# Two attention phases on one core: the parts of the softmax maxima made on VectorE instead of GpSimd, and a first phase with another lead and later fills

## The chip, the core and the metric

The program runs on one core of a Trainium2 chip. The metric is device time in microseconds (us) of one execution. The engines are TensorE (PE, matrix multiplications and transposes), VectorE (DVE), ScalarE (ACT), GpSimd (POOL) and SyncE (SP, which issues the transfers here). Each engine walks its own list of instructions in order; semaphores order them among the engines.

## The reference

Four layers work on x of 16 batches x 256 tokens x 128 features, with a context of 16 x 1601 x 128 and a condition of 16 vectors. Layer 0 is self attention with modulated layer norm and a gate, then cross attention to the normalized context, then an MLP with gelu. Layer 1 is a small mixture of experts. Layer 2 is cross attention to the normalized context. Layer 3 is self attention, cross attention and an MLP. All attention has 16 heads of 8 features:

```python
attn_w = softmax(einsum('bhqd,bhkd->bhqk', q, k) * scale, axis=-1)
attn_out = einsum('bhqk,bhkd->bhqd', attn_w, v)
x = x + gate_a[:, None] * (attn_out @ W_proj + b_proj)
...
c_attn_w = softmax(einsum('bhqd,bhsd->bhqs', q_c, k_c) * scale, axis=-1)   # 1601 keys
x = x + c_attn_out @ W_cproj + b_cproj
x = x + gate_m[:, None] * (gelu(x_norm2 @ W_mlp1 + b_mlp1) @ W_mlp2 + b_mlp2)
```

The softmax is over 256 keys in self attention and 1601 keys in cross attention, and it needs the maximum of each row of scores.

## The kernel before

The program has four stages after one another: `modulation` (condition vectors through weights), `attention_phase` "pa" (layer 0), `expert_layer` (layer 1), `attention_phase` "pb" (layers 2 and 3). Each attention phase has two streams of batches: z, self attention with 256 keys, and c, cross attention with 1601 keys. In pa each has 16 batches, and c's batch reads x after z's same batch. In pb c has 32 (16 of layer 2, 16 of layer 3), z has 16 between them.

**How a phase is ordered.** `body_plan` (L221) writes the plan of one *body*: a list of tokens, each with a position from 0 to 1, the stream and an offset in batches. `stage_list` (L314) repeats the plan body after body and drops what doesn't exist. In body b a token with offset `off` works on batch b + off + lead of its stream; the lead of c is 0, that of z 4 in pa and −4 in pb. So pa begins with bodies that hold only z's attention (batches 0 to 3, while c's first batches are being prepared), then has 12 with both, then four with c's attention alone. Every engine walks the same list, so a token's position fixes its place in each in-order queue.

**The tokens.** `S`/`T` are score matmuls (PE L890), `exp` on ACT L668, `V` the product with the values (PE L914). `M` computes scores once more, with queries on partitions, for the maxima: a matmul on PE (L927) into one of three banks (`dbank`), and a maximum along the row on DVE (L599). 60% of a batch's `M` (M_LEAD) lie in the body before its scores, the rest in the body itself; two batches' maxima are thus always in flight. When the four pairs of heads of one half are done, `Rn` follows:
- DVE reduces over the segments and negates: `negm`, 128x16 (L604).
- POOL casts it to bf16 (`mbf`, L815), copies that back to f32 (`mhl`, first part, L817) and subtracts it from `negm` (second part, L818).

Then `Rt`: PE transposes `mhl` (L935, waits for both parts), ACT writes it as bf16 rows (L728), and `mr` on SP (L526) copies these as additional rows of the stacked queries, where the score matmul subtracts the maximum. In pa `Rn` stands at positions 0.8135 and 0.3135 for z (half 0 and 1) and 0.8798 and 0.3798 for c, and `Rt` of c's half 1 at 0.4188.

**What prepares a batch.** `ldx` (L273) loads x and, where the norm is modulated, `acols`, its columns; `ln` is the layer norm (statistics on DVE L610 and L613, the rest on POOL L770 to L778); `xt` and `q` transpose it and project; `ctx`, `k` and `v` do so for the keys and values; POOL splits q and k into bf16 parts (L803 among them), and `kq` (SP L515, 12 transfers for q and 12 for k) stacks them. For c `ldx` stands at 0.700 with offset 3, `ln` at 0.080, `xt` at 0.150, `q` at 0.200 with offset 2. **What ends a batch**: `o`, `ot`, `proj`, `ln2`, `x2t`, `h` (POOL makes the polynomial of gelu in three 128x1024 instructions, L848, L850, L852), `tanh`, `gm`, `fc2`, `st` (store; z at 0.450, c at 0.600).

**Fills.** At the start of a phase DVE and POOL fill the tiles that need ones or zeros (stacked queries and keys of both streams, the values' column of ones, the output bank; DVE from L550). DVE then waits for all weights (L565) and permutes them. One semaphore counts all fills (N_SET); PE waits for it before the first token, SP before each `kq`.

Of the kernel before, what the change touches and what calls it, by code (L numbers as in the profile page):

```python
# [17 lines left out]
ALU = mybir.AluOpType  # L18
# [3 lines left out]
P = 128  # L22
# [198 lines left out]
def body_plan(streams):  # L221
# [46 lines left out]
    for s in streams:  # L268
# [4 lines left out]
        at(0.700, 3, "ldx")  # L273
        at(0.720, 0, "ldr")
        at(0.080, 2, "ln")
        if s.has_ctx:
            at(0.705, 3, "ldc")
            at(0.150, 2, "xt")
            at(0.200, 2, "q")
# [20 lines left out]
        else:  # L300
            at(0.240, 2, "xt")
# [12 lines left out]
def stage_list(streams):  # L314

    plan = body_plan(streams)
# [3 lines left out]
    for b in range(first, last + 1):  # L320
        for s, off, tok in plan:
            i = b + off + s.lead
            if 0 <= i < len(s.items):
                spec = s.items[i][0]
                if tok[0] in ("cs", "ca") and not spec.ctx_ln:
                    continue
                if tok[0] in ("ln2", "x2t", "h", "tanh", "gm", "fc2") and not spec.mlp:
                    continue
                out.append((tok, s, i))
# [6 lines left out]
def attention_phase(nc, nm, streams, cols_d, rows_d, ident_d):  # L336

    PROG = stage_list(streams)
# [36 lines left out]
    with Semaphores(nc) as sems, ExitStack() as ctx:  # L375
# [27 lines left out]
        for s in streams:  # L403
# [31 lines left out]

            s.x_in, s.a_cols, s.c_in = sem(f"{m}_x_in"), sem(f"{m}_a_cols"), sem(f"{m}_c_in")
# [13 lines left out]
        consts, ones_set, v_zero, biases = sem("consts"), sem("ones_set"), sem("v_zero"), sem("biases")  # L450
        tailed = [s for s in streams if s.last < P]
# [7 lines left out]
        N_SET = 6 * len(streams) + 4 * len(tailed) + 1  # L459

        @block.sync
        def _(sp):
# [24 lines left out]
            for tok, s, i in PROG:  # L487
                k, (spec, n), w = tok[0], s.items[i], i % 2
                if k == "ldx":
# [5 lines left out]
                    if spec.q_cols or spec.k_cols:  # L495
                        if i:
                            sp.wait_ge(a_free, a_done(("xt",), s, i - 1))
                            if s.has_ctx:
                                sp.wait_ge(a_free, a_done(("ctx", len(s.groups) - 1), s, i - 1))
                        sp.dma_start(s.acols[:], cols_d[n]).then_inc(s.a_cols, 16)  # L500
# [6 lines left out]
                elif k == "kq":  # L507
                    sp.wait_ge(ones_set, N_SET)
# [39 lines left out]
        def _(dve):  # L548
            for s in streams:
                dve.memset(s.kst[0][:], 1.0).then_inc(ones_set, 1)  # L550
                for i in range(2):
                    full = s.kt - 1 if s.last < P else s.kt
                    dve.memset(s.vaug[i][:, 0:full], 1.0).then_inc(ones_set, 1)
                    if s.last < P:
# [1163 lines left out]
```

## Time and profile before

| | us |
|---|---|
| median of 3 runs | 5723.09 (5717.75 to 5727.13) |
| the profiled execution | 5719.91 |
| its span, first to last instruction | 5718.1 |
| PE busy | 4820.5 |
| DVE busy | 3989.6 |
| ACT busy | 3680.6 |
| POOL busy | 1669.9 |

The profile counts as busy the time of instructions alone. A busy PE isn't PE at its peak, and a group's idle time is the time in which the engine stood before that group, put down to the semaphore event that ended it. The phases take about 36 to 2000 us (pa), 2000 to 2560 (experts) and 2560 to 5718 (pb) of the span.

### The profile page before, as it was taken

Reading aid. Unit: us, or ns where it says so; the run is one execution under the profiler, and the core shown is the slowest. Engines: PE = TensorE matmul, PEld = TensorE weight load, DVE = VectorE, ACT = ScalarE, POOL = GpSimd, SP = SyncE. Lnnn points to the kernel's source line nnn. Section 1 sums busy time; section 2 is a strip of 40 time slices with the busy share of each in tenths; the row PEclk is TensorE's granted clock in tenths of the full one; section 3 lists DMA queues with packets and bytes.
Section 4 is the critical chain, followed back from the end, with each engine's and each line's share of the span. In section 5 each row is a group of like instructions: output and inputs, shape, how many; then the busy total and the mean of one; then the engine's idle time right before and its main releaser. Section 6 shows DMA issues by size and latency. Waiting matters only on the chain.

```text
span 5718.1 us, 123215 instructions
## 1 busy us (share of the span) xinstructions
PE 4820.5 (84%) x47956; PEld 2303.5 (40%) x47956; DVE 3989.6 (70%) x8517; ACT 3680.6 (64%) x5027; POOL 1669.9 (29%) x2691
## 2 busy tenths in 40 slices
PE   3688888888888688876888888888888998888887
PEld 1233333333343267762333333343434443344333
DVE  3487777787777344445888787887777777777774
ACT  1366776676766444432777777777777776667666
POOL 2424334334322100013232423233222323222221
PEclk9699999999999899996999999999999999999998
DMA  1221111112110111111122111121212121111110
GB/s 42 64 61 44 51 54 50 52 46 58 44 52 26 37 30 32 32 28 57 46 59 60 55 49 56 51 64 51 64 52 59 39 59 43 50 40 51 40 44 7
DMA packets 362975, 271.11 MB, mean 47 GB/s; under 512 B 47911, under 2 KB 325002, under 8 KB 362396
## 3 DMA queue, kind: packets, MB, share of 16 engines
q1 hardware_dynamic: 362396, 263.23, 16.2%
q8 instruction: 383, 6.28, 0.5%
q14 instruction: 196, 1.61, 0.1%
HBM read 86.96 MB, written 12.78 MB: 17 GB/s over the span
## 4 chain that ended last, share of the span: by engine, by line
PE 32%; DVE 8%; ACT 6%; POOL 4%; issue 4%; SPq 0%; DMA 0%; ACTq 0%; POOLq 0%
PE pb_obank L914 12%; PE pb_dbank L927 8%; DVE pb_c_maxs L599 6%; ACT pb_probs L668 4%; PE pb_aunit L890 4%; PE pb_aunit L961 2%; PE pb_aunit L968 2%; POOL pb_c_cin L789 1%; PE pb_aunit L1001 1%; PE pb_dbank L975 1%; DVE pb_z_maxs L599 1%; POOL pb_c_hg L852 1%; PE pb_aunit L995 1%; POOL pb_c_cs_y L785 1%; ACT pb_c_ksp L712 1%
## 5 line engine op out<-in xcount | busy, mean ns | idle before, releaser
L599 DVE TENSOR_REDUCE pb_c_maxs<-pb_dbank 128x1 f32<-128x512 f32 (+1 forms) x3584 | 2048.7, 626 | 659.3 <-PE pb_dbank L927 646.6
L668 ACT ACTIVATE pb_probs<-pb_aunit 128x1024 f32<-128x1024 f32 (+1 forms) x1792 | 1756.5, 1025 | 465.3 <-PE pb_aunit L890 370.2
L599 DVE TENSOR_REDUCE pa_c_maxs<-pa_dbank 128x1 f32<-128x512 f32 (+1 forms) x1792 | 1027.6, 626 | 392.7 <-PE pa_dbank L927 387.4
L668 ACT ACTIVATE pa_probs<-pa_aunit 128x1024 f32<-128x1024 f32 (+1 forms) x960 | 942.9, 1025 | 260.4 <-PE pa_aunit L890 188.0
L927 PE MATMUL pb_dbank<-pb_c_kst,pb_c_qst 62*128 62x512 bf16 (+1 forms) x4096 | 886.5, 346 | 139.7 <-DVE pb_c_maxs L599 75.5
L914 PE MATMUL pb_obank<-pb_probs,pb_c_vaug 128*9 128x256 f32 x13312 | 893.2, 383 | 6.5 <-ACT pb_probs L668 6.3
L890 PE MATMUL pb_aunit<-pb_c_qst,pb_c_kst 64*128 64x256 bf16 x6144 | 597.9, 274 | 53.2 <-ACT pb_probs L668 21.3
L927 PEld LDWEIGHTS pb_dbank<-pb_c_kst,pb_c_qst 62*128 62x128 bf16 x4096 | 249.0, 94 | 778.8 <-DVE pb_c_maxs L599 561.0
L927 PE MATMUL pa_dbank<-pa_c_kst,pa_c_qst 62*128 62x512 bf16 (+1 forms) x2048 | 447.6, 353 | 62.8 <-DVE pa_c_maxs L599 24.2
L914 PE MATMUL pa_obank<-pa_probs,pa_c_vaug 128*9 128x256 f32 x6656 | 461.8, 393 | 1.1 <-ACT pa_probs L668 1.0
L914 PEld LDWEIGHTS pb_obank<-pb_probs,pb_c_vaug 128*9 128x9 f32 x13312 | 276.6, 90 | 377.2 <-issue 184.4
L890 PEld LDWEIGHTS pb_aunit<-pb_c_qst,pb_c_kst 64*128 64x128 bf16 x6144 | 258.5, 95 | 244.1 <-ACT pb_probs L668 80.4
L890 PE MATMUL pa_aunit<-pa_c_qst,pa_c_kst 64*128 64x256 bf16 x3072 | 299.3, 277 | 26.3 <-ACT pa_probs L668 17.0
L927 PEld LDWEIGHTS pa_dbank<-pa_c_kst,pa_c_qst 62*128 62x128 bf16 x2048 | 123.1, 94 | 391.0 <-DVE pa_c_maxs L599 255.7
L599 DVE TENSOR_REDUCE pa_z_maxs<-pa_dbank 128x2 f32<-128x512 f32 x256 | 163.9, 685 | 114.3 <-PE pa_dbank L927 112.8
L914 PEld LDWEIGHTS pa_obank<-pa_probs,pa_c_vaug 128*9 128x9 f32 x6656 | 140.3, 91 | 195.9 <-issue 101.9
L803 POOL TENSOR_TENSOR pb_c_kf<-pb_c_kf,pb_c_ksp 128x1024 f32<-128x1024 f32 x64 | 114.4, 1787 | 315.7 <-ACT pb_c_ksp L712 315.7
L890 PEld LDWEIGHTS pa_aunit<-pa_c_qst,pa_c_kst 64*128 64x128 bf16 x3072 | 128.9, 96 | 116.6 <-ACT pa_probs L668 44.3
L599 DVE TENSOR_REDUCE pb_z_maxs<-pb_dbank 128x2 f32<-128x512 f32 x256 | 164.3, 684 | 10.3 <-PE pb_dbank L927 8.7
L770 POOL TENSOR_SCALAR pb_c_rs_v<-pb_c_agg 128x2 f32<-128x2 f32 x32 | 7.9, 246 | 491.0 <-DVE pb_c_agg L613 490.9
L815 POOL CAST pb_c_mbf<-pb_c_negm 128x16 bf16<-128x16 f32 x64 | 12.7, 198 | 411.0 <-DVE pb_c_negm L604 411.0
L961 PE MATMUL pb_aunit<-pb_c_srct,pb_l_cross_wkp 128*128 128x512 f32 (+1 forms) x256 | 122.6, 609 | 7.8 <-ACT pb_probs L668 7.8
(475 smaller groups left out, 6607.0 us busy)
## 6 DMA issues: line engine op xcount, KB each, us to landing
pb_c_kst<-pb_c_ksp SPq DMA_DIRECT2D x384, 200.1 KB
pa_c_kst<-pa_c_ksp SPq DMA_DIRECT2D x192, 200.1 KB
pb_c_cin<-in_ctx SPq DMA_DIRECT2D x32, 768.0 KB
pa_c_cin<-in_ctx SPq DMA_DIRECT2D x16, 768.0 KB
moe_cin<-in_ctx SPq DMA_DIRECT2D x16, 768.0 KB
pb_c_qst<-pb_c_qsp SPq DMA_DIRECT2D x384, 32.0 KB
pa_z_qst<-pa_z_qsp SPq DMA_DIRECT2D x192, 32.0 KB
pa_z_kst<-pa_z_ksp SPq DMA_DIRECT2D x192, 32.0 KB
```

What stands on the lines that cost most here:

```text
L599: dve.tensor_reduce(dst, dbank[N % RING_D][:, 0:cnt * width].rearrange("p (s c) -> p s c", s=cnt), AX.X, ALU.max).then_inc(d_free, 1)
L668: act.activation(probs[u % RING_P][0:rows].rearrange("p a i q -> p (a i q)"), src[0:rows, :], ACT.Exp, scale=HD ** -0.5).then_inc(a_free, 1)
L712: act.activation(s.ksp[:, 0, at:at + width], src[:, 0:width], ACT.Identity, bias=w.bk[:]).then_inc(a_free, 1)
L785: pool.tensor_tensor(s.cs_y[:], s.cs_v[:], mhalf[:, 0:s.kt], ALU.pow).then_inc(s.c_p, 1)
L789: pool.tensor_scalar(s.cin[0:rows, t, :], s.cin[0:rows, t, :], s.cs_m[0:rows, t:t + 1], s.cs_y[0:rows, t:t + 1], ALU.add, ALU.mult).then_i ...
L803: pool.tensor_tensor(s.kf[:, part], s.kf[:, part], s.ksp[:, 0, part], ALU.subtract).then_inc(s.k_r, 1)
L852: pool.tensor_tensor(s.hg[:], s.hg[:], s.z[:], ALU.mult).then_inc(s.g_p, 1)
L890: ins = pe.matmul(dst[:, par * 512 + h * NQ:par * 512 + (h + 1) * NQ], s.kst[b2][lo:lo + ROWS, pair, t * P:(t + 1) * P], s.qst[b2][lo:lo + ...
L914: ins = pe.matmul(obank[32 * h4:32 * h4 + HD + 1, half * NQ:(half + 1) * NQ], s.vaug[i % 2][:, t, 4 * q + h4, :], src, start=(t == 0), sto ...
L927: ins = pe.matmul(dbank[nd[tok, s.key, i, par] % RING_D][:, col:col + width], s.qst[b2][lo:lo + MAX_ROW, p, qt * P:(qt + 1) * P], s.kst[b2 ...
L961: ins = pe.matmul(dst[:, at - t0 * P:at - t0 * P + width], w.wkp[:], src[:, at:at + width], start=True, stop=True)
L968: ins = pe.matmul(dst[0:rows, (t - t0) * P:(t - t0 + 1) * P], (s.srct if s.has_ctx else s.xmt)[:, t * P:t * P + rows], w.wv[:], start=True ...
```

## The change

Three things are changed. First, `Rn`'s cast, copy and subtraction are issued by DVE right behind `negm`, in both phases, and no longer by POOL. Second, in pa z's lead is 3 instead of 4, and c's `ldx`, `ln`, `xt`, `q` stand at 0.500, 0.620, 0.700, 0.760 with offset 2 (`late_x`); the load of `acols` becomes a token of its own, `lda`, in both phases. Third, fills are counted for each stream; the output bank comes first and PE waits for it alone, `kq` and the first `v` wait for their stream's fills, and in pa c's fills stand behind z's second layer norm on DVE and POOL. In pb only the order of the fills changes.

```diff
-def body_plan(streams):
+def body_plan(streams, late_x):
...
-        at(0.700, 3, "ldx")
         at(0.720, 0, "ldr")
-        at(0.080, 2, "ln")
         if s.has_ctx:
+            if late_x:
+                at(0.500, 2, "ldx")
+                at(0.620, 2, "ln")
+                at(0.700, 2, "xt")
+                at(0.760, 2, "q")
+            else:
+                at(0.700, 3, "ldx")
+                at(0.080, 2, "ln")
+                at(0.150, 2, "xt")
+                at(0.200, 2, "q")
+            at(0.701, 3, "lda")
             at(0.705, 3, "ldc")
-            at(0.150, 2, "xt")
-            at(0.200, 2, "q")
...
         else:
+            at(0.700, 3, "ldx")
+            at(0.701, 3, "lda")
+            at(0.080, 2, "ln")
...
# SP
                 elif k == "kq":
-                    sp.wait_ge(ones_set, N_SET)
+                    sp.wait_ge(s.filled, s.fills)
...
# DVE
+            def fill(s):
+                dve.memset(s.kst[0][:], 1.0).then_inc(s.filled, 1)
+                full = s.kt - 1 if s.last < P else s.kt
+                for i in range(2):
+                    dve.memset(s.vaug[i][:, 0:full], 1.0).then_inc(s.filled, 1)
+                    if s.last < P:
+                        dve.memset(s.vaug[i][0:SET_ROWS, full], 1.0).then_inc(s.filled, 1)
+                        dve.memset(s.vaug[i][SET_ROWS:P, full], 0.0).then_inc(s.zeroed, 1)
+                if s.last < P:
+                    dve.wait_ge(s.zeroed, 2)
+                    for i in range(2):
+                        dve.memset(s.vaug[i][SET_ROWS:s.last, full], 1.0).then_inc(s.filled, 1)
+
+            dve.memset(obank[:], 0.0).then_inc(ones_set, 1)
             for s in streams:
...
+                if s.key not in fill_late:
+                    fill(s)
...
                     dve.tensor_reduce(s.negm[half][:]..., AX.X, ALU.max, negate=True).then_inc(s.m_neg, 1)
+                    dve.wait_ge(s.m_neg, 2 * i + half + 1)
+                    if i:
+                        dve.wait_ge(a_full, a_done(("Rt", half), s, i - 1))
+                    dve.tensor_copy(s.mbf[half][:], s.negm[half][:]).then_inc(s.m_bf, 1)
+                    dve.wait_ge(s.m_bf, 2 * i + half + 1)
+                    dve.tensor_copy(s.mhl[half][:, :, :, 0, :], s.mbf[half][:]).then_inc(s.m_hl, 1)
+                    dve.tensor_tensor(s.mhl[half][:, :, :, 1, :], s.negm[half][:], s.mbf[half][:], ALU.subtract).then_inc(s.m_hl, 1)
...
+                for o in streams:
+                    if fill_late.get(o.key) == (k, s.key, i):
+                        fill(o)
...
# ACT, before the first v
+                    if i == 0 and tok[1] == 0:
+                        act.wait_ge(s.filled, s.fills)
...
# POOL: fill(s) in the same manner (the two stacked queries and the second K tile); Rn is gone
-                elif k == "Rn":
...
# PE
-            pe.wait_ge(ones_set, N_SET)
+            pe.wait_ge(ones_set, 1)
...
-    attention_phase(nc, "pa", [Stream("c", S, batches(l0_cross), 0), Stream("z", NQ, batches(l0_self), 4)], cols, rows, ident)
+    attention_phase(nc, "pa", [Stream("c", S, batches(l0_cross), 0), Stream("z", NQ, batches(l0_self), 3)], cols, rows, ident, True, {"c": ("ln", "z", 1)})
...
-    attention_phase(nc, "pb", [Stream("c", S, batches(l2_cross) + batches(l3_cross), 0), Stream("z", NQ, batches(l3_self), -4)], cols, rows, ident)
+    attention_phase(nc, "pb", [Stream("c", S, batches(l2_cross) + batches(l3_cross), 0), Stream("z", NQ, batches(l3_self), -4)], cols, rows, ident, False, {})
```

## Rows read from the trace of the kernel before

**Rows 1.** the page: busy time of each engine, its share of the span, instructions
```profile
PE 4820.5 (84%) x47956; PEld 2303.5 (40%) x47956; DVE 3989.6 (70%) x8517; ACT 3680.6 (64%) x5027; POOL 1669.9 (29%) x2691
```

**Rows 2.** --tile pa_c_mhl: engine idle before it until that releaser; us, times
```profile
  POOL pa_c_mhl L818: 45.8, 16
```

**Rows 3.** --tile pb_c_mhl: the same, second attention phase
```profile
  POOL pb_c_mhl L818: 13.9, 23
```

**Rows 4.** --timeline, TensorE, first phase; start, us, engine, line, work, [idle before]
```profile
670.36 0.39 PE L927 MATMUL pa_dbank<-pa_c_kst,pa_c_qst 62*128 62x512 bf16 x2
674.10 0.41 PE L935 MATMUL pa_aunit<-pa_ident,pa_c_mhl 128*16 128x128 f32 x2 [3.35 <-POOL pa_c_mhl L818]
...
684.50 0.39 PE L935 MATMUL pa_aunit<-pa_ident,pa_z_mhl 128*16 128x128 f32 x2
```

**Rows 5.** --timeline, TensorE, second phase, a body with both streams and an MLP
```profile
4354.90 0.39 PE L927 MATMUL pb_dbank<-pb_c_kst,pb_c_qst 62*128 62x512 bf16 x2
...
4363.30 0.39 PE L935 MATMUL pb_aunit<-pb_ident,pb_z_mhl 128*16 128x128 f32 x2
```

**Rows 6.** --timeline, GpSimd (POOL), same stretch as rows 4
```profile
667.92 1.90 POOL L848 TENSOR_TENSOR pa_c_hg<-pa_c_z 128x1024 f32<-128x1024 f32 x1
...
671.04 2.34 POOL L852 TENSOR_TENSOR pa_c_hg<-pa_c_hg,pa_c_z 128x1024 f32<-128x1024 f32 x1
...
673.74 0.22 POOL L818 TENSOR_TENSOR pa_c_mhl<-pa_c_negm,pa_c_mbf 128x16 f32<-128x16 f32 x1
```

**Rows 7.** --timeline, VectorE (DVE), same stretch as rows 4
```profile
668.02 0.22 DVE L604 TENSOR_REDUCE pa_c_negm<-pa_c_maxs 128x16 f32<-128x64 f32 x1
```

**Rows 8.** --windows: busy us of each engine (instructions), PEclk, DMA share, GB/s
```profile
674.00:686.00 12.00, 10.01 (x67) 3.77 (x67) 5.23 (x9) 6.53 (x8) 1.65 (x3) 0.72 0.04 13
706.00:717.00 11.00, 10.32 (x132) 3.97 (x130) 10.47 (x19) 8.08 (x11) 0.00 (x0) 1.00 0.01 3
...
3480.00:3518.00 38.00, 34.85 (x427) 13.53 (x425) 35.39 (x64) 29.56 (x36) 4.31 (x9) 1.00 0.14 35
```

**Rows 9.** --timeline, SP's queue: first transfers of bodies, ramp and end of phase one
```profile
132.88 7.90 SPq L515 DMA_DIRECT2D pa_z_qst<-pa_z_qsp  x12
...
167.44 7.90 SPq L515 DMA_DIRECT2D pa_z_qst<-pa_z_qsp  x12
...
214.20 7.90 SPq L515 DMA_DIRECT2D pa_c_qst<-pa_c_qsp  x12
...
1382.44 8.44 SPq L515 DMA_DIRECT2D pa_c_qst<-pa_c_qsp  x12
...
1491.24 8.97 SPq L515 DMA_DIRECT2D pa_c_qst<-pa_c_qsp  x12
...
1688.94 7.90 SPq L515 DMA_DIRECT2D pa_c_qst<-pa_c_qsp  x12
...
1781.54 7.90 SPq L515 DMA_DIRECT2D pa_c_qst<-pa_c_qsp  x12
```

**Rows 10.** --timeline, VectorE, start of the first phase
```profile
38.82 10.73 DVE L550 MEMSET pa_c_kst<- 128x12808 bf16 x1 [9.79 <-issue]
...
58.06 0.21 DVE L570 COPY pa_l_cross_wqp<-pa_probs 128x64 f32<-128x64 f32 x1
...
62.55 0.49 DVE L610 BATCH_NORM_STATS2 pa_z_stats<-pa_z_xin 128x6 f32<-128x128 f32 x2
```

**Rows 11.** --timeline, SP's queue: the last load before the first layer norm
```profile
45.30 0.43 SPq L494 DMA_DIRECT2D pa_z_xin<-in_x  x1
```

**Rows 12.** --lines by form, VectorE: busy us, mean ns; PSUM copy, SBUF cast, smallest
```profile
L1252 DVE COPY moe_pt<-moe_bank_u 128x512 f32<-128x512 f32 x32 | 21.9, 684 | 1.7 <-PE moe_bank_u L1597 1.7
...
L1331 DVE CAST moe_brows<-moe_brest 1x512 bf16<-1x512 f32 x2 | 0.8, 418 | 0.1
...
L1366 DVE TENSOR_SCALAR moe_nm<-moe_nm 128x1 f32<-128x1 f32 x32 | 4.9, 154 | 1.1
```

**Rows 13.** --source L803, GpSimd: duration min/median/max ns, first and last start
```profile
L803 POOL TENSOR_TENSOR pa_c_kf<-pa_c_kf,pa_c_ksp x32: 1279/1705/2536, 197.8 to 1751.2; 128x1024 f32<-128x1024 f32 x16, 128x577 f32<-128x577 f32 x16
```

More of the change, by code:

```diff
@@ L311, in body_plan, with stage_list @@
     return [t for _, t in marks]
-def stage_list(streams):
-    plan = body_plan(streams)
+def stage_list(streams, late_x):
+    plan = body_plan(streams, late_x)
     first = min(-3 - s.lead for s in streams)
@@ L326, in stage_list @@
                     continue
+                if tok[0] == "lda" and not (spec.q_cols or spec.k_cols):
+                    continue
                 if tok[0] in ("ln2", "x2t", "h", "tanh", "gm", "fc2") and not spec.mlp:
@@ L333, with attention_phase @@
 ACT_RING = ("S", "T", "xt", "q", "ctx", "k", "v", "Rt", "ot", "proj", "x2t", "h", "fc2")
-def attention_phase(nc, nm, streams, cols_d, rows_d, ident_d):
-    PROG = stage_list(streams)
+def attention_phase(nc, nm, streams, cols_d, rows_d, ident_d, late_x, fill_late):
+    PROG = stage_list(streams, late_x)
     na, nd, ns, nv, no, out_before, values_before = {}, {}, {}, {}, {}, {}, {}
@@ L434, in attention_phase @@
                 s.x2a, s.x2 = sb(f"{m}_x2a", [P, QT, D]), sb(f"{m}_x2", [P, QT, D])
+            s.filled, s.zeroed = sem(f"{m}_filled"), sem(f"{m}_zeroed")
+            s.fills = 6 if s.last == P else 10
             s.x_in, s.a_cols, s.c_in = sem(f"{m}_x_in"), sem(f"{m}_a_cols"), sem(f"{m}_c_in")
@@ L448, in attention_phase @@
             s.d_lin2, s.d_x2, s.x_out = sem(f"{m}_d_lin2"), sem(f"{m}_d_x2"), sem(f"{m}_x_out")
-        consts, ones_set, v_zero, biases = sem("consts"), sem("ones_set"), sem("v_zero"), sem("biases")
-        tailed = [s for s in streams if s.last < P]
+        consts, ones_set, biases = sem("consts"), sem("ones_set"), sem("biases")
         a_full, a_free = sem("act_ring_full"), sem("act_ring_free")
@@ L494, in _ @@
                     sp.dma_start(s.xin[:], spec.x_src[n].rearrange("(t p) d -> p t d", p=P)).then_inc(s.x_in, 16)
[L495 to L500, printed above, removed]
+                elif k == "lda":
+                    if i:
+                        sp.wait_ge(a_free, a_done(("xt",), s, i - 1))
+                        if s.has_ctx:
+                            sp.wait_ge(a_free, a_done(("ctx", len(s.groups) - 1), s, i - 1))
+                    sp.dma_start(s.acols[:], cols_d[n]).then_inc(s.a_cols, 16)
                 elif k == "ldc":
@@ L758, in _, with fill @@
         def _(pool):
+            def fill(s):
+                for i in range(2):
+                    pool.memset(s.qst[i][:], 0.0).then_inc(s.filled, 1)
+                pool.memset(s.kst[1][:], 1.0).then_inc(s.filled, 1)
+            pool.memset(mhalf[:], -0.5)
             for s in streams:
-                for i in range(2):
-                    pool.memset(s.qst[i][:], 0.0).then_inc(ones_set, 1)
-                pool.memset(s.kst[1][:], 1.0).then_inc(ones_set, 1)
-            pool.memset(mhalf[:], -0.5)
+                if s.key not in fill_late:
+                    fill(s)
             for tok, s, i in PROG:
@@ L861, in _ @@
                     pool.tensor_tensor(s.x2[:], s.x2a[:], s.x1[:], ALU.add).then_inc(s.d_x2, 1)
+                for o in streams:
+                    if fill_late.get(o.key) == (k, s.key, i):
+                        fill(o)
         @block.tensor
```

22 lines of the change are left out of this document (1 added, 21 removed).

## The prediction

> **What bounds the kernel.** I read the page first. Over the span TensorE (PE) is busy 84%, VectorE (DVE) 70%, ScalarE (ACT) 64%, GpSimd (POOL) 29% [rows 1]. PE sets the pace, DVE stands close behind it, POOL has room. The windows sharpen this: in the dense stretch of a body of the first phase PE works 10.32 of 11 us and DVE 10.47 of 11, in one of the second phase PE 34.85 and DVE 35.39 of 38 [rows 8]. So wherever the maxima pass, DVE is as full as PE, and whatever is added to it there shows.
>
> Next the waits of the tile that the change touches, the two parts of the maxima (mhl). PE idled 45.8 us until POOL had made those of the cross stream in the first phase, 16 times [rows 2], and 13.9 us, 23 times, in the second [rows 3]. The timeline shows one: PE's last maxima matmul starts at 670.36, the transpose of mhl only at 674.10, after 3.35 us of waiting [rows 4]. DVE had the negated maxima at 668.24 (668.02 + 0.22) [rows 7], but POOL was in its three gelu instructions, of which the last runs from 671.04 to 673.38, and wrote mhl at 673.74 [rows 6]. The small work stands in POOL's in-order queue behind 128x1024 work. The stall has an echo. From that last maxima matmul to the z stream's transpose it takes 684.50 − 670.36 = 14.14 us here; the same work without a wait takes 4363.30 − 4354.90 = 8.40 in the second phase [rows 4, 5]. Of the 5.74 us between them 3.35 are the wait; the other 2.4 fit the granted clock, 0.72 on average from 674 to 686 where dense stretches show 1.00 [rows 8]: part of that stretch ran at the 1.2 GHz level, after PE had sat idle, instead of 2.4.
>
> The length of each kind of body is read on SP's queue, from the first stacking transfer of one body to that of the next: with the self stream alone 167.44 − 132.88 = 34.6 us, with both streams and the MLP 1491.24 − 1382.44 = 108.8, with the cross stream alone 1781.54 − 1688.94 = 92.6 [rows 9].
>
> **The change part by part**, against the profiled execution, 5719.91 us with a span of 5718.1.
>
> A. *The parts leave POOL.* mhl then depends on nothing but DVE. What is late next is DVE's own three instructions, some 0.5 us behind 668.24, at about 668.8, before PE's last maxima matmul of 670.36 even starts. So the wait goes: **−45.8 us**.
>
> B. *The clock behind it.* In the 12 bodies that hold both streams and an MLP, at 2.4 us each: **−29 us**.
>
> C. *Second phase.* The same edit there removes most of 13.9 us; I count **−12**. These waits are short (0.6 us each), so I take no clock for them.
>
> D. *DVE's new work.* Each half of each batch adds two copies and a subtraction of 128x16: 2 x 16 x 2 = 64 sets in the first phase, 2 x 48 = 96 in the second, 160 in all. Before shows no such operation on DVE. Nearest rows: its smallest instruction 0.154 us [rows 12], the reduction of 128x64 in front of these 0.22 [rows 7]. Three of them make 0.46 to 0.66; two wait for the one before on their own engine, which could carry it to 0.9. I take 0.5, nearest to the smallest row, since 16 elements are little. It isn't below nothing: DVE gives nothing up. 76 sets (half 0 of the 80 batches' turns in both phases, less four in the ramp) fall into the dense stretches, where nearly no idle time takes them up: I charge three quarters, 76 x 0.5 x 0.75 = 28. The other 84 stand beside PE's own transposes and projections, where DVE is 5.23 of 12 us busy [rows 8]: a fifth, 8. Together **+36**. What is queued behind the new waits on DVE is the next maxima reductions; PE waits for these with only three banks in the ring, so the cover is about one reduction deep. Without cover: 160 x 0.5 = 80.
>
> E. *Cross stream's x late.* Its load, layer norm, transpose and q projection move to 0.50, 0.62, 0.70 and 0.76 of a body, all into the dense stretch. The new places move 0.75 us on DVE (0.49 of statistics [rows 10] and an aggregation of about half that), one ring slot each of PE and ACT; nothing is added. Price between −16 (1 us per body less at the crowded start) and +24 (1.5 more in the dense part, twice DVE's 0.75); as DVE is full there I take **+8**. On SP's queue the load now stands right behind the self stream's store, whose landing it waits for (the same batch), and ahead of the transfers of the next maxima rows; between 0.50 and the next body's stacking SP has only loads and stores to issue, so a few us of waiting there cost nothing. The loads of the modulation columns keep their place; as tokens of their own they cost nothing.
>
> F. *One ramp body less.* With the self stream three ahead, a body that held only it disappears: **−34.6**. The cross stream's first x hangs closer behind the first self output: output, store, load, statistics, POOL's norm, transpose. That chain now ends inside a short body. I allow 2.5 us of PE waiting: **−32** in sum.
>
> G. *The other end.* The work stays the same, so one cross-only body turns into one with both: +108.8 − 92.6 = +16.2. That body sheds the stall and its echo too, 5.7. A cross-only one had about 2: 45.8 less 12 x 3.35 leaves 1.4 of stall for each of four, and some echo. So 3.7 more is shed: **+12.4** (16.1 before rounding).
>
> H. *Fills.* DVE starts a 10.73 us fill of the cross stream's K tile at 38.82 and first permutes weights at 58.06 [rows 10]; the last load that matters was issued at 45.30 [rows 11]. Its landing has no row. Bounds: 45.7 (its issue over) to 58.06, so −12.3 to 0. I take 48.3, 3 us for a small transfer: **−9.8**. The cross stream's fills then run behind the second layer norm of the self stream. Their cover is the time until that stream's K and Q are loaded, projected, split and stacked; before that DVE has no maxima to reduce. If the cover were gone it would cost up to 16 us, and the term would be about +6.
>
> The sum: −45.8 − 29 − 12 + 36 + 8 − 32 + 12.4 − 9.8 = −72.2. 5719.9 − 72.2 = 5647.7. The median of the runs stands 3.2 above the profiled one (5723.09), so I predict **5651**.
>
> *A rule against it.* GpSimd's subtraction takes 1.279 us at the shortest (577 elements) and 2.536 at the longest (1024): a factor of 1.98 where the sizes make 1.77, so its length seems to vary with what runs beside it; and DVE's cast from SBUF of 512 takes 0.418 us where a copy from PSUM takes 0.684 [rows 12, 13]: SBUF to SBUF is in a faster mode. Both are seen here; whether a small DVE instruction is held up whole is not. The Trainium skill ("SBUF — State Buffer", section "Who interferes with whom") says that DVE and GpSimd share one pair of ports as an exclusive lock, taken by DVE in its two-port modes and when it has two SBUF inputs, so that a clash blocks the whole instruction. By it all three new instructions could stand behind a gelu instruction of POOL's, and the sum would come out as in the next part; without it, as above.
>
> **Rivals.**
> 1. *DVE stands behind POOL's long instructions* (0.27). At 668.24 POOL is in a 1.90 us instruction that began at 667.92, and two more follow, the last of 2.34 [rows 6]. If one DVE instruction waits for the first of them to end (669.82) and another for a part of the next, DVE loses 1.6 to 5 us, and with it the maxima behind. At 1.6 to 2.5 half of the 5.74 us remains: 13 x 2.87 = 37 less gained, 5688. For it: the varying lengths. Against it: DVE and POOL overlap all through, and the maxima read PSUM.
> 2. *The shorter ramp doesn't pay* (0.15). If PE waits for the late x chain in each body, E takes +24 and more, and F shrinks by another 15: 5680 or so. For it: the chain has 0.12 of a body, 13 us, from load to norm, but only 4 us in a ramp body. Against it: a transfer of 3 us and a norm fit into 13.
> 3. *DVE's work reaches PE in full* (0.08), and the kernel gets slower. At 0.9 us a set, none of it covered, D is 160 x 0.9 = 144, against 108.2 from all other terms: +36, 5759. It decides from 108.2 / 160 = 0.68 us per set on PE's path. For it: DVE is as full as PE [rows 8] and the ring has three banks. Against it: half of the sets stand where DVE has room.
>
> **How the numbers follow.** The forecast has 0.50. Its low end: D with 0.46 a set, E at −16, the fills at −12.3 and a little more of C give 5616, and with the clock better elsewhere 5605. Its high end: D at 65 (0.9 a set by the same shares), E at +24: 5696. Rivals 1 and 2 lie within that; 5702 leaves out rival 3 and some of rival 1's deep end. So 5605 to 5702. About 0.2% (11 us) is what can be told from no change. Faster: all of the forecast and nine tenths of rivals 1 and 2, 0.88; within 0.2%: 0.05; slower: 0.07, most of rival 3 and the far end of 1.
>
> **What would show it.** No wait on POOL's mhl ahead of PE's transpose; the granted clock at 1.00 between the last maxima matmul and the z transpose, 8.4 us apart; DVE's three new instructions at 0.15 to 0.22 us each (rival 1: some over 1 us, those of the cross stream's half 1 in the first phase); full bodies of about 104 us; one self-only body less, the first cross stacking some 40 us earlier; the first layer norm near 52.8 rather than 62.55. The second phase is the control for D: by D and C it should be longer by 10 to 25 us, since 96 of 160 sets are there. If it is longer by over 50, rival 3 is right; if it isn't longer at all, D was an overestimate. Full bodies over 107 would say that A and B failed.

## The result

The changed kernel takes 5643.17 us (median of 4 runs, 5640.68 to 5645.99) against 5723.08 (4 runs). The ratio is 0.9861, 95% interval 0.9844 to 0.9878: faster by 1.2 to 1.6%. Forecast were 5651 us and a range of 5605 to 5702. Measured again on another chip, the ratio was 0.9872 (0.9843 to 0.9902). Runs of the kernel before fall into two groups, 5688 to 5704 us and 5711 to 5731 us, and its four runs above and its profiled execution (5719.91) are of the second: against that group the gain is some 80 us, against the first 54 to 57 (the changed kernel's ten runs lie between 5637 and 5646). So ratios taken on different chips can't be compared to 0.1%, and the traces carry most of what follows. A trace is a single execution, though: that of the parts alone (first experiment) is the fastest of its six, 8 us below their median, and this is said where it matters.

The page of the changed kernel, busy us by engine, share of the span, instructions [against rows 1]:

```profile
PE 4780.1 (85%) x47956; PEld 2291.1 (41%) x47956; DVE 4091.3 (73%) x8997; ACT 3681.7 (65%) x5027; POOL 1579.2 (28%) x2211
```

DVE has 480 instructions more, 160 sets of three, and is busy 101.7 us longer: 0.64 us a set. PE did the same 47956 matmuls in 40 us less, and its mean granted clock was 0.959 instead of 0.945.

The tile of the parts, first the cross stream's in the first phase, then in the second: who waited until DVE had written it [against rows 2 and 3].

```profile
  PE pa_aunit L961: 1.8, 1
...
  PE pb_aunit L961: 1.9, 1
```

The 45.8 us of waits in the first phase are 1.8, the 13.9 of the second 1.9. Part of this comes back at another place. DVE's new work stands ahead of its next reductions, and PE's maxima matmuls wait longer for a free bank. Here are these waits (us in total, times, longest), first before, then after:

```profile
PE pb_dbank L927 <- DVE pb_c_maxs L599: 111.5, 220, 1.3
PE pa_dbank L927 <- DVE pa_c_maxs L599: 48.8, 102, 1.4
```

```profile
PE pb_dbank L953 <- DVE pb_c_maxs L615: 127.5, 262, 1.5
PE pa_dbank L953 <- DVE pa_c_maxs L615: 64.9, 145, 1.5
```

They rose by 16 us in each phase, 32 in all, where 56 us of waits on the parts went.

SP's queue, first transfers of bodies [against rows 9]: the first body with the cross stream, then three full ones.

```profile
170.05 7.90 SPq L527 DMA_DIRECT2D pa_c_qst<-pa_c_qsp  x12
...
781.16 8.23 SPq L527 DMA_DIRECT2D pa_c_qst<-pa_c_qsp  x12
...
887.37 8.74 SPq L527 DMA_DIRECT2D pa_c_qst<-pa_c_qsp  x12
...
992.79 7.90 SPq L527 DMA_DIRECT2D pa_c_qst<-pa_c_qsp  x12
```

The cross stream's first stacking is at 170.05 instead of 214.20: 44.2 us earlier. Full bodies are 106.2 and 105.4 here, 105.6 on average where before they were 109.2. DVE starts its first layer norm 10.3 us earlier (52.24 against 62.55), and runs the cross stream's long fill behind the second one [against rows 10]:

```profile
52.24 0.49 DVE L633 BATCH_NORM_STATS2 pa_z_stats<-pa_z_xin 128x6 f32<-128x128 f32 x2
...
61.07 10.73 DVE L562 MEMSET pa_c_kst<- 128x12808 bf16 x1 [2.62 <-issue]
```

The fills end at 76.8, and DVE then waits 2.75 us for PE's first maxima of the self stream at 79.52: they are covered. The first phase ends where SP loads the expert layer's first x. That is at 1904.47 (1973.58 before):

```profile
1904.47 0.38 SPq L1288 DMA_DIRECT2D moe_xin<-x_after  x1
```

So the first phase gave 69.1 us. From there to the second phase's first stacking nothing changed (632.4 against 632.1), and from that stacking to the end it is 5642.0 − 2536.9 = 3105.1 against 5718.1 − 2605.7 = 3112.4: 7.3 us less. Together 76.1 of span.

**What DVE's instructions meet.** DVE and POOL in one full body of the first phase:

```profile
830.03 0.22 DVE L620 TENSOR_REDUCE pa_c_negm<-pa_c_maxs 128x16 f32<-128x64 f32 x1
830.29 0.99 DVE L625 CAST pa_c_mbf<-pa_c_negm 128x16 bf16<-128x16 f32 x1
831.31 0.17 DVE L627 CAST pa_c_mhl<-pa_c_mbf 128x16 f32<-128x16 bf16 x1
831.39 1.02 DVE L628 TENSOR_TENSOR pa_c_mhl<-pa_c_negm,pa_c_mbf 128x16 f32<-128x16 f32 x1
```

```profile
829.35 1.90 POOL L871 TENSOR_TENSOR pa_c_hg<-pa_c_z 128x1024 f32<-128x1024 f32 x1
831.34 1.05 POOL L873 TENSOR_SCALAR pa_c_hg<-pa_c_hg 128x1024 f32<-128x1024 f32 x1
832.47 2.34 POOL L875 TENSOR_TENSOR pa_c_hg<-pa_c_hg,pa_c_z 128x1024 f32<-128x1024 f32 x1
```

A cast of 128x16 takes 0.99 us and ends at 831.28, where POOL's first gelu instruction ends (831.25). The subtraction takes 1.02 and ends at 832.41, POOL's second ends at 832.39. The first copy back (831.31) starts in the gap between the two and takes 0.17. In the last two bodies with an MLP the cast runs into the third gelu instruction and takes 1.99. Over all of them (duration min, median, max):

```profile
L625 DVE CAST pa_c_mbf<-pa_c_negm x32: 174/175/1994, 252.6 to 1833.6; 128x16 bf16<-128x16 f32 x32
```

This is rival 1's mechanism, and what the Trainium skill ("SBUF — State Buffer", section "Who interferes with whom") says of the lock, seen instruction by instruction. In the first phase 13 casts and 13 subtractions start inside one of POOL's gelu instructions, in the second 15 casts; each of them ends 0.02 to 0.04 us after it. POOL's own durations didn't change (2.34 before and after). PE's transposes hardly waited for it (1.8 and 1.9 us above); PE's maxima matmuls did, and part of their 32 us is this lock.

**The clock that is left.** In the second phase's bodies with the cross stream alone the length was 92.1 to 92.2 us before (the first, 93.9, apart). Now it is 89.1 or 91.6 (two are 92.3 and 93.3). Windows that start at the same piece of work in a body of 91.5 us, in one of 89.1, and of before (busy us by engine, then PEclk):

```profile
4783.90:4795.40 11.50, 10.93 (x106) 6.21 (x107) 6.06 (x10) 7.84 (x10) 6.66 (x7) 0.75 0.14 33
...
4875.40:4886.90 11.50, 10.46 (x133) 5.08 (x130) 8.04 (x14) 9.52 (x12) 6.61 (x7) 1.00 0.27 75
```

```profile
4937.10:4948.60 11.50, 10.93 (x93) 6.07 (x96) 5.37 (x9) 7.19 (x10) 6.14 (x7) 0.68 0.14 37
```

The waits ahead of it are the same in the first two (0.57 and 1.26 us on maxima). In one PE then goes on partly at 1.2 GHz, in the other wholly at 2.4. That is worth 2.5 us. Why the one falls and the other doesn't, no run here shows. It isn't that PE stood idle less. In these bodies the wait on POOL's parts had been 0.2 us each, and PE's idle time went up, from 8.6 us a body to 9.1 (the bodies of 91.5) or 9.5 (those of 89.1), 0.4 of it in front of maxima matmuls.

### The profile page after: what moved, and what is told of

The parts are those of the page before. It is cut to its first block, busy times and chain, and to the rows that moved or that the text cites. A ratio compares the mean times of both kernels' runs of the same rounds, so it can differ in the third digit from the quotient of the medians.

```text
span 5642.0 us, 123219 instructions
## 1 busy us (share of the span) xinstructions
PE 4780.1 (85%) x47956; PEld 2291.1 (41%) x47956; DVE 4091.3 (73%) x8997; ACT 3681.7 (65%) x5027; POOL 1579.2 (28%) x2211
## 4 chain that ended last, share of the span: by engine, by line
PE 33%; DVE 10%; ACT 7%; issue 4%; POOL 1%; SPq 0%; DMA 0%; ACTq 0%; POOLq 0%
PE pb_obank L940 12%; PE pb_dbank L953 8%; DVE pb_c_maxs L615 7%; ACT pb_probs L694 5%; PE pb_aunit L916 4%; PE pb_aunit L987 2%; PE pb_aunit L994 2%; PE pb_aunit L979 1%; DVE pb_z_maxs L615 1%; PE pb_aunit L1027 1%; PE pb_dbank L1001 1%; PE pb_aunit L1021 1%; PE pb_aunit L970 1%; ACT pb_c_ksp L738 1%; PE pb_aunit L924 0%
## 5 line engine op out<-in xcount | busy, mean ns | idle before, releaser
L953 PE MATMUL pb_dbank<-pb_c_kst,pb_c_qst 62*128 62x512 bf16 (+1 forms) x4096 | 897.8, 343 | 153.7 <-DVE pb_c_maxs L615 91.5
L940 PEld LDWEIGHTS pa_obank<-pa_probs,pa_c_vaug 128*9 128x9 f32 x6656 | 138.8, 90 | 188.4 <-issue 91.5
L953 PE MATMUL pa_dbank<-pa_z_kst,pa_z_qst 62*128 62x256 bf16 x512 | 71.1, 297 | 61.5 <-DVE pa_c_maxs L615 28.5
L987 PE MATMUL pb_aunit<-pb_c_srct,pb_l_cross_wkp 128*128 128x512 f32 (+1 forms) x256 | 114.3, 574 | 10.4 <-ACT pb_probs L694 10.4
```

Of the source, the lines that this page charges most:

```text
L940: ins = pe.matmul(obank[32 * h4:32 * h4 + HD + 1, half * NQ:(half + 1) * NQ], s.vaug[i % 2][:, t, 4 * q + h4, :], src, start=(t == 0), sto ...
L953: ins = pe.matmul(dbank[nd[tok, s.key, i, par] % RING_D][:, col:col + width], s.qst[b2][lo:lo + MAX_ROW, p, qt * P:(qt + 1) * P], s.kst[b2 ...
L987: ins = pe.matmul(dst[:, at - t0 * P:at - t0 * P + width], w.wkp[:], src[:, at:at + width], start=True, stop=True)
```

## Experiments

Each was timed in 5 rounds beside the kernel before. Times are medians; ratios are to the kernel before on the same chip.

**The parts alone.**

```diff
# on the kernel before: POOL's Rn taken out; on DVE behind negm
+                    dve.tensor_copy(s.mbf[half][:], s.negm[half][:])
+                    dve.tensor_copy(s.mhl[half][:, :, :, 0, :], s.mbf[half][:])
+                    dve.tensor_tensor(s.mhl[half][:, :, :, 1, :], s.negm[half][:], s.mbf[half][:], ALU.subtract)
```

> The kernel before with one edit: DVE makes the two parts of the maxima, in both phases; lead 4, old places of the cross stream's x, fills all at the start. Theory (the stall behind GpSimd and the clock behind it pay, less DVE's new work): terms A to D of the prediction, -45.8 - 29 - 12 + 36 = -51 us, so about 5672; the trace of the changed kernel, with full bodies 3.3 us shorter and a second phase 7 us shorter, makes it -12 x 3.3 - 4 x 2 - 7 = -55. Rival (DVE held behind GpSimd's gelu instructions eats half of it): -25 to -30, 5695. Rival 2 (the parts pay nothing and the ramp is all): within 10 us of before. The casts of half 1 of the cross stream on DVE should show about 1 us or more in the full bodies of the first phase.

5654.79 us, ratio 0.9916 (0.9896 to 0.9935). The first phase ends at 1910.39, 63.2 us before that of the kernel before; the second phase is 10.4 us shorter; the span is 5644.6. A full body, from one first transfer to the next:

```profile
706.86 8.82 SPq L515 DMA_DIRECT2D pa_c_qst<-pa_c_qsp  x12
810.80 8.29 SPq L515 DMA_DIRECT2D pa_c_qst<-pa_c_qsp  x12
```

It takes 103.9 us, as eight of the full bodies do, less than the 105.6 of the whole change. Inside the body the cross stream's transpose of the maxima comes 2.7 us earlier than before, the self stream's 5.4 (60.2 against 65.6 us from the stacking), close to the 5.74 of the prediction. The 2.7 is less than the wait of 3.35 that went, because the maxima in front of it now come later: PE's waits for a bank rose by 12.0 us in this phase and 16.9 in the second, from the parts alone. The granted clock from 500 to 1400 us is 1.00, against 0.96 before. The casts take 0.575 us on average here too, so the lock was there and the gain came all the same. Rival 2 (the ramp is all) is out. By the medians the gain is 47 us against this chip's runs of before, just under the theory's 51 to 55; by the traces it is 73.5.

**All but the parts.**

```diff
# on the changed kernel: Rn's three instructions back on POOL, DVE's taken out
```

> The changed kernel with the parts of the maxima back on GpSimd: lead 3, cross stream's x late, its fills late. Theory: terms E to H without the shed stall: +8 - 32 + 16.1 - 9.8 = -18 us against before, about 5705, with one more stall of 3.35 us and its clock. Rival (the parts carry little, the ramp nearly all): -60 or more, 5660. Rival (ramp doesn't pay): 5723 or above. If the two groups of edits are independent, this and the run with the parts alone add up to the whole change, -80.

5689.85 us, ratio 0.9972 (0.9954 to 0.9990). By the trace (5701.92 us) the first phase ends 21.3 us earlier and the second isn't shorter. Theory: −18. The two halves give −63.2 and −21.3 in the first phase, together −84.5, where the whole change gives −69.1. So by the traces they are not independent: 15 us of one are lost when the other is there. The size of this isn't shown, since the trace of the parts alone is 8 us faster than their median, and by the times nothing is lost: the two ratios add up to −1.12%, the whole change has −1.28 to −1.39%.

**Lead four again.**

```diff
-Stream("z", NQ, batches(l0_self), 3)
+Stream("z", NQ, batches(l0_self), 4)
```

> The changed kernel with the self stream four batches ahead in the first phase instead of three; all else as changed (parts on DVE, cross stream's x late, fills late). Theory: the ramp body comes back (+34.5) and one full body turns into one of the cross stream alone (105.5 - 96 = -9.5 or so): +20 to +25 against the changed kernel, about 5665. Rival (late x waits on the self stream's output, which a lead of three makes tight): 5643 or less, since a lead of four takes that wait away in every body.

5669.32 us, ratio 0.9940 (0.9921 to 0.9959). The first phase ends at 1926.07, 21.6 us later than with three: the theory's 20 to 25. (By the medians it is 26 to 28, on another chip than the changed kernel's.) The full bodies stay at 105.5, so the lead is not what makes them longer than 103.9.

**Fills early.**

```diff
-rows, ident, True, {"c": ("ln", "z", 1)})
+rows, ident, True, {})
```

> The changed kernel with the cross stream's fills back at the start of the first phase. Theory (term H): DVE fills for 16 us before it permutes the weights; the first layer norm starts some 10 us later and all behind it: +10 us, 5653. Rival (the fills behind the second layer norm of the self stream delay its first maxima as much as they would at the start): 0, 5643; the trace then has the cross stream's first stacking near 170 us as in the changed kernel, by theory near 180.

5651.89 us, ratio 0.9909 (0.9890 to 0.9927). The first cross stacking is at 179.38 instead of 170.05 (9.3 us), but the first phase ends only 4.3 us later (6.2 after that of the changed kernel's second trace). The first two bodies caught up with 1.2 of it. Most of the rest goes with the clock: three later full bodies of this execution are 104.6 us long at a clock of 1.00, where the changed kernel's are 105.4 to 106.2 at 0.98. By the medians the kernel is 8.7 to 10.4 us slower, as the theory said, though on another chip. So term H is right; that it is worth less at the end of the phase isn't shown.

**The change once more, gelu later, the parts twice, x in the next body**, all on one chip.

> The changed kernel itself once more, beside the three below, so that they can be compared with it and with the kernel before on one chip. Both theories: the ratio of the first measurement, 0.986 (within its interval); the runs of single parts (-0.84% for the parts of the maxima alone, -0.28% for all else alone) would add up to only 0.9888.

5641.54 us, ratio 0.9872 (0.9843 to 0.9902); the same bodies as the first time, and the first phase ends at 1902.62, 1.9 us earlier: that much two traces of one kernel can differ.

```diff
-            at(0.325, -1, "h")
+            at(0.375, -1, "h")
# tanh, gm, fc2, st: each 0.05 later as well
```

> The changed kernel with gelu's steps 0.05 of a body later (h 0.375, tanh 0.470, gm 0.530, fc2 0.590, store 0.650), so that GpSimd isn't in its 128x1024 instructions when DVE makes the cross stream's parts of half 1. Theory (DVE stands behind GpSimd's instruction: its cast and its subtraction take 0.99 and 1.02 us in 10 full bodies where others take 0.17): both fall to 0.17 to 0.2, DVE gets back 1.7 us in each full body of the first phase and 0.8 to 1.8 in each body with an MLP of the second, and the time falls by up to 13 x 1.7 + 15 x 0.9 = 35 us if PE follows DVE there, by 10 to 15 if only part of it was on PE's path. Rival (the long casts are work of DVE itself or hidden): the durations stay, or they fall and the time stays within 5 us.

5653.19 us, ratio 0.9894 (0.9867 to 0.9921): 12 us slower than the changed kernel. The lock went away as the theory said:

```profile
L625 DVE CAST pb_c_mbf<-pb_c_negm 128x16 bf16<-128x16 f32 x64 | 11.7, 183 | 2.4 <-DVE pb_c_negm L620 0.2
```

0.183 us on average against 0.395, and in the first phase 0.175 against 0.562. The cross-only bodies of the second phase fell from 90.6 to 88.8 us on average, and the second phase by 14.3 us (5644.5 − 2553.7 = 3090.8). PE's waits for a bank of the maxima fell from 127.5 to 107.8 us there, which is what the lock had cost PE, if the later gelu did nothing else to them. In the first phase they fell from 64.9 to 57.4, but those behind the self stream's maxima rose from 15.4 to 19.9. It did do something else: the full bodies of the first phase grew from 105.6 to 107.7, with the clock still at 0.98. In those at a clock of 1.00 (106.4 us, against 104.5 in the changed kernel) PE waits 1.05 us until ACT has written the self stream's rows of maxima and 0.72 until it has written gelu's input (12.6 and 11.4 us over the phase, against 3.0 and none). So what DVE's 1.7 us a body were worth in the first phase can't be read from this run. (The execution that was traced is the fastest of its six, 7 us below their median.)

```diff
+                    dve.tensor_copy(s.mbf2[half][:], s.negm[half][:])          # scratch tiles
+                    dve.tensor_copy(s.mhl2[half][:, :, :, 0, :], s.mbf2[half][:])
+                    dve.tensor_tensor(s.mhl2[half][:, :, :, 1, :], s.negm[half][:], s.mbf2[half][:], ALU.subtract)
```

> The changed kernel with DVE's three small instructions issued twice for each half, the second set into scratch tiles that nobody reads. Measures term D: the price of a set. Theory as predicted (0.5 us a set, three quarters of it on the path in dense stretches, a fifth elsewhere): +36 us, 5679. From the traces (a full body lost only 0.2 to 0.4 us to the sets of half 0): 160 x 0.1 = +15. Rival 3 of the prediction (DVE's work reaches PE in full, 0.9 a set): +80 to +140.

5751.19 us, ratio 1.0062 (1.0041 to 1.0082): 110 us for 160 more sets, 0.69 us each, and the kernel is slower than before. The second set is dearer than the first: a cross-only body of the second phase pays 0.6 us for two sets, one with both streams 1.2 to 2.8 for four (100.8 to 102.4 against 99.6), a full body of the first phase 5.0 on average. There the second set's copy back runs into POOL's third, longest instruction, 13 times, and takes 2.31 us each time:

```profile
L634 DVE CAST pa_c_mhlx<-pa_c_mbfx 128x16 f32<-128x16 bf16 x32 | 33.4, 1043 | 1.1
```

```profile
PE pa_dbank L960 <- DVE pa_c_maxs L618: 102.3, 158, 3.6
```

The wait of PE's maxima matmuls on DVE rises from 64.9 to 102.3 us in the first phase and from 127.5 to 146.3 in the second, and the clock fell: most full bodies of the first phase stand at 0.95 instead of 0.98. So the loss that rival 3 of the prediction feared is there for a second set, but not for the reason alone that it gives: 69 of the 99 us by which the traces differ lie in the first phase, where POOL holds DVE up.

```diff
-                at(0.700, 2, "xt")
-                at(0.760, 2, "q")
+                at(0.150, 1, "xt")
+                at(0.200, 1, "q")
...
-        at(0.000, 1, "kq")
+        at(0.270 if s.has_ctx and late_x else 0.000, 1, "kq")
```

> The changed kernel, but the cross stream's transpose and q projection stand at 0.150 and 0.200 of the body after its layer norm (offset 1) instead of 0.700 and 0.760, and its stacking at 0.270 instead of 0. In body time this is where they stood before, one batch later. Theory (term E: late x costs 1.6 us in each full body because PE, ACT and DVE are full there; a body is 103.9 us with the old places and 105.6 with the new): bodies of 104, 13 x 1.6 = 21 us less than the changed kernel, about 5622. Rival (the longer body comes from the lead of three or from the stacking's place): bodies stay at 105 to 106 or grow since the stacking at 0.270 comes just before the maxima that need it; no gain.

5794.21 us, ratio 1.0141 (1.0114 to 1.0169). The theory had left out that the token stacks K too:

```profile
PE pa_dbank L953 <- DMA pa_c_kst<-pa_c_ksp: 147.8, 15, 13.8
```

24 transfers of 0.6 us from 0.27 of the body end too late for the maxima at 0.4; PE waited for them 15 times, 9.9 us each. This says nothing of the place of xt and q, so it was tried again:

**Only Q late; old places with late fills; two instructions.**

```diff
# on the changed kernel: xt 0.100, q 0.140 (offset 1); K stacked at 0, Q at 0.220
+        at(0.000, 1, "kk")
+        at(0.220 if s.has_ctx and late_x else -0.001, 1, "kq")
```

> The changed kernel with the cross stream's transpose and q projection at 0.100 and 0.140 of the next body, and its stacking split: the twelve transfers of K stay at 0, the twelve of Q follow at 0.220. In the run before it, with both at 0.270, PE waited 147.8 us for the stacked K. Theory (late x costs because it stands in the dense part; the Ks were what came too late): no wait for K, bodies of 104 us, 5620 to 5628. Rival (the transfers of Q are late as well): waits on the stacked Q of 1 us or more in each body, no gain or a loss.

5640.58 us, ratio 0.9864 (0.9846 to 0.9882): like the changed kernel. PE waits for the stacked Q once, 15.9 us at the start of the cross stream, and in no full body, and the bodies are 105.6 all the same. So taking the transpose and the projection out of the dense part didn't make them shorter, and my theory of term E falls.

```diff
# on the changed kernel
-batches(l0_self), 3)], cols, rows, ident, True,
+batches(l0_self), 4)], cols, rows, ident, False,
```

> The changed kernel with the self stream's lead of four and the cross stream's x at its old places; what is left of the change is the parts on DVE and the late fills. Theory: the run with the parts alone had full bodies of 103.9 us and ended its first phase at 1910 us (changed kernel 1904.5, with bodies of 105.6); the late fills take some 10 us off its start, so the first phase ends near 1900, 4 us ahead of the changed kernel, and the time is about 5638. So lead and late x together give nothing (ramp -34.5, the longer bodies +13 x 1.6, a cross-only body turned into a full one +8). Rival (lead and late x are worth 15 to 25 us, as terms E to G say): 5660.

5643.43 us, ratio 0.9871 (0.9853 to 0.9889), the same as the changed kernel, with bodies of 103.9 (three of 105.4 to 105.7) and the first phase ending at 1908.78. So beside the parts on DVE the shorter lead and the late x pay nothing together: 22 us from the lead, and as much given back by the late x. That price can be read from two runs that differ in it alone, this one and the one with a lead of four again: there the first phase ends at 1926.07, 17.3 us later, and the median is 26 us higher (on another chip). What the late fills give is seen less well. The first phase ends 1.6 us before that of the parts alone (1910.39), but this trace is the slowest of its five runs and that one the fastest of its six; by the medians it is 11 us, again on two chips.

```diff
-                    dve.tensor_reduce(s.negm[half][:]...
+                    dve.tensor_reduce(s.mhl[half][:, :, :, 0, :]...   # first part unrounded
-                    dve.tensor_copy(s.mhl[half][:, :, :, 0, :], s.mbf[half][:])
```

> The changed kernel with two instructions instead of three for the parts: the reduction writes the negated maxima straight into the place of the first part (ScalarE rounds it to bf16 when it writes the rows anyway), DVE then casts and subtracts. Theory (a second set of three cost 0.69 us, of which most in the places where it hit another of GpSimd's long instructions): 160 x 0.2 = 32 us less busy time on DVE, 5 to 15 us less in the time. Rival (the first set lies in DVE's slack): within 5 us of the changed kernel.

5639.89 us, ratio 0.9868 (0.9847 to 0.9889). The span of the profiled execution, the fastest of its five, is 9.4 us below the changed kernel's (the first phase ends at 1894.03), the median 1.7 us below: no difference that can be told in the time. PE's waits for a bank of the maxima stayed as they were (64.9 and 128.0 us).

**Two instructions, and gelu later in the second phase alone.**

```diff
# two instructions, and in the second phase alone:
+            gelu_late = 0.0 if late_x else 0.05
-            at(0.325, -1, "h")
+            at(0.325 + gelu_late, -1, "h")      # tanh, gm, fc2, st alike
```

> The two edits that shortened a trace, together on the changed kernel: DVE's two instructions instead of three in both phases, and gelu's steps 0.05 of a body later in the second phase alone (there the bodies of the cross stream with an MLP fell from about 90.4 to about 88.7 us, while in the first phase the full bodies grew from 105.6 to 107.5). Theory: the second phase 14 us shorter, the first 5 to 10: 5620, 20 us under the changed kernel, ratio 0.983 to before. Rival (in the time, two instructions gave nothing, and gelu's gain in the second phase is as uncertain): 5640, no difference from the changed kernel. GpSimd's long instructions should no longer hold DVE's cast in the second phase; in the first they still do.

5629.62 us (5626.47 to 5636.32), ratio 0.9848 (0.9821 to 0.9876). No run of it was as slow as the fastest of the changed kernel (5636.69), but the intervals of the ratios overlap, and it was not run on the changed kernel's chip. By the medians it is 12 to 14 us faster than the changed kernel, where 20 were expected; that it is faster is likely, not shown. Its first phase ends at 1898.24, 6 us before the changed kernel's, and its second phase is 5627.7 − 2529.6 = 3098.1 long, 7 us under the changed kernel's, half of what the run with gelu later had shown. Its cross-only bodies are 88.8 us on average, as in that run.

## Why the prediction came out

The sum was −72.2, the traces say −76.1. The mechanism of the main terms (A, B, F, H) is borne out, but that the sum is so close is partly luck, because two terms were off in opposite directions, E and the clock of the second phase: the first phase was forecast at −82 (A, B, E to H and 14 of D) and gave −69.1; the second at +10 (22 of D less C) and gave −7.3.

- **A, the waits: right.** 45.8 forecast, 44.0 gone. DVE's parts were ready when PE came, in spite of the lock: in the body above they end at 832.41, and PE's transpose starts at 833.38.
- **B, the clock behind them: right** in the body: the self stream's transpose came 5.4 us earlier with the parts alone, 5.74 forecast for wait and clock. From PE's matmul at 832.37, the one ahead of the transpose, to the self stream's transpose at 841.46 it is 9.1 us (8.4 forecast).
- **C, second phase: the wait right (12.0 gone), the clock left out.** I took none because the waits were 0.6 us each. That mean hid two kinds: nine waits of 0.9 us in bodies with both streams, a dozen of 0.2, nearly all in cross-only ones, and two longer ones at the end. The clock changed in the latter. From the first cross-only body on, eleven bodies lost 17.8 us (ten of them 92.3 to 90.6 on average), with only 2 us of such waits in them, while PE's idle time grew. So this gain is clock, and it isn't the echo of the removed wait that term B describes. That it comes from where the parts are made is shown (the parts alone have these bodies too, all but the parts has 92.2 throughout); how, isn't. This is the term that was mis-sized by most: it was put at nothing.
- **D, DVE's new work: right in size.** A set takes 0.64 us (0.5 taken, bounds 0.46 to 0.9). PE's waits for a bank rose by 32 us (+36 taken). In the second phase a body with four sets and no wait to lose became 1.3 longer (97.6 to 98.9, layer 3), and one that lost a wait of 0.9 us still 0.2 longer (99.4 to 99.6, layer 2). So four sets cost 1.1 to 1.3 us of such a body. All bodies ahead of the cross-only ones together grew by 11.6 us, where D less C says 10. The prediction says that D was an overestimate if the second phase isn't longer at all, and it is 7.3 shorter; but that sign misleads, since the cross-only bodies' clock, which C left out, hides D's cost. The split that I gave, three quarters in dense stretches and a fifth elsewhere, isn't tested by this: some 37 us of DVE's 101.7 are the cross stream's casts and subtractions behind POOL, which D didn't have.
- **E, x late: sign right, size off.** +8 taken, bounds −16 to +24. Full bodies are 105.6 with it and 103.9 without: 1.7 in each of ten bodies, 17 us, twice what I took, and the two runs that differ in it alone say 17.3 for the phase. About half of it goes with the clock. Here are two full bodies of the changed kernel and one of the parts alone, with the same 1007 matmuls in each (length, then busy us by engine, then PEclk):

```profile
464.48:569.04 104.56, 91.74 (x1007) 41.61 (x1003) 85.70 (x192) 76.94 (x102) 39.72 (x57) 1.00 0.19 54
675.08:781.16 106.08, 93.31 (x1007) 42.11 (x1003) 85.74 (x192) 76.95 (x102) 39.71 (x57) 0.98 0.18 53
```

```profile
706.86:810.80 103.94, 91.75 (x1007) 41.70 (x1003) 85.81 (x192) 76.67 (x102) 39.86 (x57) 1.00 0.20 54
```

  At a clock of 1.00 late x costs 0.6 us a body, which is what the 8 us that I took come to. But only two full bodies of the changed kernel keep that clock. The nine behind them have 0.98, where with the parts alone a single one has. In the body from 887.37 the dip stands near 950 us:

```profile
949.40:952.40 3.00, 2.82 (x19) 1.11 (x16) 2.08 (x6) 2.98 (x4) 2.85 (x3) 0.56 0.18 52
```

  In the body before it there is none there, and one of 0.83 to 0.91 from 801 to 814. Moving the transpose and the projection away didn't help. What is common to the runs with such bodies is the load at 0.500 and the layer norm at 0.620; whether it is they, or the gap at the old place, wasn't tried, and what brings the dips back stays open.
- **F and H, ramp and fills: right to 2 us** at the first stacking (−44.2; −41.8 forecast). H is 9.3 at the first stacking (9.8 taken) and 9 to 10 by the medians; the loads of the self stream's x took 2.0 to 3.2 us to land in the changed kernel, where I took 3. F with G is 21.6 (19.6 forecast; G's own sum, 16.2 less 3.7, makes 12.5 and not 12.4).
- **Rival 1 (0.27)** described what DVE does (1.7 us lost in the body shown, of the 1.6 to 5 that it names), and its price was wrong: in the body of the parts alone 5.4 of the 5.74 were gained, where it says half. But the lock isn't free. With gelu moved out of its way PE's waits for a bank fell by 19.7 us in the second phase, which was 14.3 us shorter in one run and 7.0 in another; in the first phase no run shows a gain.
- **Rival 2 (0.15)**, that ramp and late x don't pay, is right beside the parts on DVE (lead four with old places is as fast), but through E's size, about half of which goes with the clock, and not through a PE that waits for x.
- **Rival 3 (0.08)** didn't come. A second set of the three instructions brings such a loss, at 0.69 us a set, where it said 0.68; but that closeness is luck, since POOL's lock, which it doesn't name, is part of the reason.

## What to carry to other kernels

A small operation that another engine waits for should not stand in an in-order queue behind large ones, even if it then runs on the busier engine: here 0.64 us a set on a DVE that is 70% busy bought 5 us of a full body (109.2 to 103.9). Charge the new work where it shows, in the waits for what stands behind it in the queue. Count with a wait also the clock that PE loses behind it, and compare like bodies at like clock before a difference is put down to an edit: 2.5 us of a body of 90 hung on it here. And before edits are bundled, time each alone: the lead and the late x gave nothing beside the first edit.

## What the runs showed of the hardware

- A DVE cast or subtraction of 128x16 between SBUF tiles that starts while POOL is in a 128x1024 instruction ends 0.02 to 0.04 us after that instruction: 0.99, 1.02, 1.99 us instead of 0.17, and 2.31 for a copy back in the run with the parts twice. A DVE instruction that starts in the gap between two of POOL's takes its 0.17. The reductions from PSUM kept their length (128x512: 683 ns mean before and after), and POOL's own lengths didn't move.
- The same waits in front of the same work left PE at 2.4 GHz in one body and took it to 1.2 GHz for some us in another (89.1 and 91.6 us, granted clock 1.00 and 0.96 over the body). Full bodies of the first phase with the same instructions are 104.5 us at 1.00 and 105.4 to 106.2 at 0.98. What decides between the two, no run here shows.
